# A filter's stored values in fp32, and its squares in a buffer of their own

## The reference

```python
x = x + _L0_conv_ref(_gn(x), w0, w1, w2, bias)   # 3 Haar levels, each a 5x5 convolution 128 -> 128 channels
x = x + _L1_conv_ref(_gn(x), spatial_weight)

# _L1_conv_ref: a 5x5 filter whose weights come from the image
dot = jnp.einsum('bchw,bckhw->bkhw', x, patches)
norm_x = jnp.sqrt(jnp.sum(x * x, axis=1))
norm_p = jnp.sqrt(jnp.sum(patches * patches, axis=1))
sim = dot / jnp.maximum(norm_x[:, None] * norm_p, EPS)
weight = (sim + 1.0) * 0.5 * spatial_weight[None, :, None, None]
out = jnp.einsum('bckhw,bkhw->bchw', patches, weight)
```

## Time and profile before

| | |
|---|---|
| median of 3 runs | 2229.93 us (2226.68 to 2234.81) |
| profiled execution | 2236.67 us, span 2235.0 us |
| busy of the span | PE 1634.4 us (73%), DVE 1408.0 (63%), ACT 738.2 (33%), POOL 448.3 (20%) |
| mean granted clock of PE | 0.829 of 2.4 GHz |
| DMA | 329.95 MB, mean 148 GB/s |

### The profile page before, as it was taken

One profiled execution on the slowest core, in us unless ns is written; L12 is line 12 of the kernel. 1 busy time (PEld: TensorE's weight loads), 2 busy tenths in 40 slices (PEclk: granted clock), 3 DMA queues, 4 the chain that ended last, 5 costly groups with the idle time before them and its releaser, 6 DMA issues.

```text
span 2235.0 us, 49426 instructions
## 1 busy us (share of the span) xinstructions
PE 1634.4 (73%) x16895; PEld 862.5 (39%) x16895; DVE 1408.0 (63%) x2121; ACT 738.2 (33%) x1222; POOL 448.3 (20%) x792
## 2 busy tenths in 40 slices
PE   5777777878578776888568785778678795875465
PEld 3543333434234343434234342335334352432243
DVE  6428646966378455966478554866479554875354
ACT  2321233423243233424233242423334242423341
POOL 1352422022301222012300232013300232011000
PEclk7888888989789897979788896989888896887566
DMA  5242446763857546673856556583766557572665
GB/s 164 75 125 75 122 129 152 185 171 92 192 141 192 140 126 167 157 186 99 189 149 183 134 133 167 140 207 99 172 162 174 139 131 178 139 197 76 146 164 135
DMA packets 151106, 329.95 MB, mean 148 GB/s; under 512 B 47092, under 2 KB 96244, under 8 KB 150260
## 3 DMA queue, kind: packets, MB, share of 16 engines
q1 hardware_dynamic: 109296, 207.18, 37.2%
q0 software_dynamic: 41472, 118.24, 20.1%
HBM read 238.70 MB, written 86.61 MB: 146 GB/s over the span
## 4 chain that ended last, share of the span: by engine, by line
PE 27%; DMA 21%; DVE 18%; SPq 17%; issue 11%; ACT 3%; DVEq 2%; POOL 0%; ACTq 0%; POOLq 0%
DMA d_n<-st_n 12%; PE conv L1300 8%; PE conv L1274 5%; DMA unit_mem<-d_n 5%; SPq L385 4%; DMA unit_mem<-d_hl 3%; SPq L413 3%; PE gram L1368 3%; PE conv L1259 3%; SPq L383 2%; PE out_ps L1393 2%; SPq L408 2%; SPq L405 2%; DVE wgt L1020 2%; PE stat_ps L1323 2%
## 5 line engine op out<-in xcount | busy, mean ns | idle before, releaser
L1020 DVE SCALAR_TENSOR_TENSOR wgt<-gram,tapw 124x512 f32<-124x512 f32 x512 | 350.4, 687 | 360.5 <-PE gram L1368 321.9
L1300 PE MATMUL conv<-thl,wconv 128*128 128x496 f16 (+2 forms) x1920 | 559.9, 422 | 16.8 <-DVE xa L899 9.6
L471 POOL DMA_DIRECT2D ring<-in_x x576 | 333.7, 584 | 475.3 <-DVE bn L781 244.1
L1368 PE MATMUL gram<-unit_mem 128*60 128x128 f16 x4096 | 264.8, 255 | 198.9 <-DMA unit_mem<-d_hl 122.8
L1368 PEld LDWEIGHTS gram<-unit_mem 128*60 128x60 f16 x4096 | 160.6, 118 | 428.9 <-issue 427.2
L1323 PE MATMUL stat_ps<-st_n,sq_c 128*128 128x306 f32 x256 | 123.0, 570 | 186.7 <-ACT st_n L556 153.7
L1300 PEld LDWEIGHTS conv<-thl,wconv 128*128 128x128 f16 x1920 | 171.2, 105 | 223.8 <-issue 81.3
L1274 PE MATMUL conv<-thl,wconv 128*128 128x480 f16 (+7 forms) x1200 | 255.3, 367 | 0.0
L1393 PE MATMUL out_ps<-wgt,vals 124*32 124x128 f32 x4096 | 195.2, 311 | 35.6 <-issue 31.5
L556 ACT ACTIVATE vals<-vals_ps 124x512 f32<-124x512 f32 x128 | 76.3, 596 | 391.5 <-PE vals_ps L1351 391.5
L505 POOL DMA_DIRECT2D up<-d_z x128 | 68.7, 539 | 560.4 <-DVE xa L951 500.5
(11 more groups left out here) (133 smaller groups left out, 2007.3 us busy)
## 6 DMA issues: line engine op xcount, KB each, us to landing
unit_mem<-d_hl SPq DMA_DIRECT2D x128, 360.0 KB, 6.5
unit_mem<-d_hl SPq DMA_DIRECT2D x256, 180.0 KB, 8.4
ring<-in_x POOLq DMA_DIRECT2D x288, 128.0 KB, 4.1
ring<-in_x POOLq DMA_DIRECT2D x288, 127.0 KB, 4.4
d_hl<-st_hl SPq DMA_DIRECT2D x128, 180.0 KB
d_v<-st_v SPq DMA_DIRECT2D x128, 180.0 KB
unit_mem<-d_v SPq DMA_DIRECT2D x64, 360.0 KB
up<-d_z POOLq DMA_DIRECT2D x160, 128.0 KB, 3.2
```

The lines of the kernel that those rows point to most:

```text
L471: pool.dma_start(dst, src).then_inc(raw_in[slot], 16)
L1020: V.scalar_tensor_tensor(out=dst, in0=g, scalar=SIM_SCALE ** 2, in1=tapw[:, :].unsqueeze(1).to_broadcast([KN, 2, 2 * QN]), op0=ALU.add, op ...
L1300: last = mm(dst[:, :, b0:b1], wconv0[:, w, 2 * (p % ROWS4) + s, dx + 2, :], thl[:, p % 2, d, s, :, b0 + dx:b1 + dx] if p % ROWS4 != 1 else ...
L1368: last = mm(bank[row:row + KQ, col:col + QN], key[:, q, e_at, TH * KW * g:TH * KW * g + KQ], tile[:, :, TH * g + 1:TH * g + 1 + TH, 1:1 + ...
```

## The change

The values go through memory once in fp32 in place of two fp16 parts: `st_v` and `d_v` are fp32, one DMA of 360 KB stores them and two DMAs load them, quadrants 0 and 1 to partitions 0 to 31 and quadrants 2 and 3 to partitions 32 to 63. The constant `pick_c` (fp32, 64x32 for each pair of quadrants, zero for the other pair) takes the place of `unpair_c`. DVE's `value_lows` is gone. The squares have a buffer of their own, `st_sq`, one for both parities; `half_in` no longer waits for the store but for `unit_low` of half h - 2; squaring is a function of its own, which waits until the matmuls of the half before have read `st_sq`; the wait for the store stands in `norms`, before the first write into `st_n`; the copy of the values follows in `norms` after the square of `st_a`. `xh2` and `xl2` now share memory with `thl`, so `wino_high(i, 0)` waits for the level-2 convolution.

```diff
-SAVES, LOADS, LATER = 80, 96, 80
+SAVES, LOADS, LATER = 64, 96, 96
...
-    unpair = np.zeros((2 * C, C), np.float16)
-    unpair[np.arange(2 * C), np.arange(2 * C) % C] = 1 / X_SCALE
+    pick = np.zeros((2 * C, 2, C), np.float32)
+    pick[np.arange(2 * C), np.arange(2 * C) // C, np.arange(2 * C) % C] = 1 / X_SCALE
...
+        xh2, xl2 = (thl[:, 0, hl, 0, 0:GR // 2, :].rearrange("p g w -> p (g w)").rearrange("p (h w) -> p h w", w=H2) for hl in range(2))
...
-        xh2, xl2 = sb("xh2", [P, H2, H2], F16), sb("xl2", [P, H2, H2], F16)
...
-        st_v = sb("st_v", [P, 2, 2, FN], F16)
+        st_v = sb("st_v", [P, 2, FN], F32)
...
+        st_sq = sb("st_sq", [P, UN], F32)
...
-                for hl in range(2):
-                    sp.dma_start(d_v[b, h, hl].rearrange("c q n -> q c n"), st_v[:, hl, h % 2, :]).then_inc(half_saved[h % 2], 16)
+                sp.dma_start(d_v[b, h].rearrange("c q n -> q c n"), st_v[:, h % 2, :]).then_inc(half_saved[h % 2], 16)
...
-                sp.dma_start(values[s][0:2 * C].rearrange("c q e n -> c (q e n)"),
-                             d_v[b, u].rearrange("l c q n -> (l c) (q n)")).then_inc(rest_in[s], 16)
+                for t in range(2):
+                    sp.dma_start(values[s][C * t:C * t + C].rearrange("c q e n -> c (q e n)"),
+                                 d_v[b, u, :, 2 * t:2 * t + 2, :].rearrange("c q n -> c (q n)")).then_inc(rest_in[s], 16)
...
             def wino_high(i, p):
                 act.wait_ge(t_wide, 8 * i + p + 1)
-                if p == 1:
-                    act.wait_ge(conv_ready, 3 * i + 3)
-                elif p or not first(i):
+                if p < 2:
+                    act.wait_ge(conv_ready, 3 * i + 1 + 2 * p)
+                if p >= 2:
                     act.wait_ge(m_ready, 16 * i + 2 * p - 2)
...
-                act.wait_ge(half_saved[half], START + SAVES * (4 * b + h // 2))
+                act.wait_ge(unit_low, START + 8 * b + (h - 1 if h >= 2 else 0))
...
                 last.then_inc(x2_done, 1)
+
+            def square_half(b, h):
                 act.wait_ge(x2_done, 8 * b + h + 1)
-                part = st_x2[:, half, :, :].rearrange("p h w -> p (h w)")
-                copy(st_n[:, half, :], part, scale=1 / X_SCALE, func=ACT.Square).then_inc(sq_done, 1)
-                copy(in_strips(st_v[:, 0, half, :]), strips(part)).then_inc(v_high, 1)
+                if h > 0:
+                    act.wait_ge(n2_ready, 16 * b + 2 * h)
+                copy(st_sq[:, :], st_x2[:, h % 2, :, :].rearrange("p h w -> p (h w)"), scale=1 / X_SCALE, func=ACT.Square)\
+                    .then_inc(sq_done, 1)
...
                 if p == 0:
                     act.wait_ge(unit_vec, START + 8 * b + h)
+                    act.wait_ge(half_saved[h % 2], START + SAVES * (4 * b + h // 2))
...
                     copy(st_b[:, :], st_a[:, :], func=ACT.Square).then_inc(root_squared, 1)
+                    copy(in_strips(st_v[:, h % 2, :]), strips(st_x2[:, h % 2, :, :].rearrange("p h w -> p (h w)"))).then_inc(v_kept, 1)
...
                     half_in(b, 0)
+                    square_half(b, 0)
                     half_in(b, 1)
...
                     norms(b, 0, 1)
+                    square_half(b, 1)
...
                     half_in(b, 2)
+                    square_half(b, 2)
...
                             half_in(b, j + AHEAD + 1)
+                            square_half(b, j + AHEAD + 1)
...
-                dve.wait_ge(value_low, 8 * b + h + 1)
+                dve.wait_ge(v_kept, 8 * b + h + 1)
...
-                mm(stat_ps[:, 0:PIECE], same_quadrant, st_n[:, h % 2, p * PIECE:(p + 1) * PIECE], start=True, stop=True)\
+                mm(stat_ps[:, 0:PIECE], same_quadrant, st_sq[:, p * PIECE:(p + 1) * PIECE], start=True, stop=True)\
...
-                                      values[s][0:2 * C, q, e, TH * KW * g:TH * KW * g + KQ], unpair_c[:, :],
+                                      values[s][0:2 * C, q % 2, e, TH * KW * g:TH * KW * g + KQ], pick_c[:, q // 2, :],
```

More of the change, by code:

```diff
@@ L130, in host_constants @@
             taps[64 * (k % 2):64 * (k % 2) + KQ, t, k // 2] = (dr == t // K - K // 2) & (dc == t % K - K // 2)
-    return square, gather, taps.reshape(KN, TAPS * 2 * QN), unpair
+    return square, gather, taps.reshape(KN, TAPS * 2 * QN), pick
 def first(n):
@@ L153, in link, with build @@
         engine.wait_ge(self.sem, self.base + self.k)
-def build(nc, x, w0, w1, w2, bias, spatial, square, gather, tapmask, unpair, out):
+def build(nc, x, w0, w1, w2, bias, spatial, square, gather, tapmask, pick, out):
     ctx = ExitStack()
@@ L196, in build @@
         gat_c = sb("gat_c", [P, Q, P], F32)
-        unpair_c = sb("unpair_c", [2 * C, C], F16)
+        pick_c = sb("pick_c", [2 * C, 2, C], F32)
         bn1, bn2 = sb("bn1", [P, CONV_TILES, 6], F32), sb("bn2", [P, CONV_TILES, 6], F32)
@@ L218, in unit_part @@
             return unit_mem[:, s, n * Q * FN:(n + 1) * Q * FN].rearrange("p (q e n) -> p q e n", q=Q, e=GROUPS)
-        keys, queries, values = ([unit_part(s, n) for s in range(2)] for n in range(3))
+        keys, queries = ([unit_part(s, n) for s in range(2)] for n in range(2))
+        values = [unit_mem[:, s, 2 * Q * FN:3 * Q * FN].bitcast(F32).rearrange("p (q e n) -> p q e n", q=2, e=GROUPS) for s in range(2)]
         norm_strips = [unit_mem[:, s, 2 * Q * FN:3 * Q * FN].bitcast(F32).rearrange("p (e n) -> p e n", e=2) for s in range(2)]
@@ L244, in build @@
         d_hl = dram("d_hl", [B, 2 * BANDS, 2, C, Q, FN], F16)
-        d_v = dram("d_v", [B, 2 * BANDS, 2, C, Q, FN], F16)
+        d_v = dram("d_v", [B, 2 * BANDS, C, Q, FN], F32)
         d_n = dram("d_n", [B, 2 * BANDS, Q, UN], F32)
@@ L298, in build @@
         sq_done = sem("sq_done")
-        v_high = sem("v_high")
+        v_kept = sem("v_kept")
         n2_ready = sem("n2_ready")
@@ L306, in build @@
         unit_high = sem("unit_high")
-        value_low = sem("value_low")
         unit_low = sem("unit_low")
@@ L372, in _ @@
             sp.dma_start(spat[:, :], spatial.rearrange("(a k) -> a k", a=1).to_broadcast([P, TAPS])).then_inc(const_in, 16)
-            sp.dma_start(unpair_c[:, :], unpair).then_inc(const_in, 16)
+            sp.dma_start(pick_c[:, :, :], pick).then_inc(const_in, 16)
             sp.wait_ge(wmixed, 7)
@@ L712, in iteration @@
                     half_in(b, 3)
+                    square_half(b, 3)
                 for j in range(CONV_TILES):
@@ L978, in units_close @@
                                        op0=ALU.mult, op1=ALU.mult).then_inc(unit_vec, 1)
-            def value_lows(b, h):
-                dve.wait_ge(v_high, 8 * b + h + 1)
-                V.tensor_tensor(in_strips(st_v[:, 1, h % 2, :]), strips(image_of(h)), in_strips(st_v[:, 0, h % 2, :]),
-                                ALU.subtract).then_inc(value_low, 1)
             def unit_lows(b, h):
                 dve.wait_ge(unit_high, 8 * b + h + 1)
-                dve.wait_ge(value_low, 8 * b + h + 1)
+                dve.wait_ge(v_kept, 8 * b + h + 1)
                 V.tensor_tensor(in_strips(st_hl[:, 1, h % 2, :]), strips(st_b[:, :]), in_strips(st_hl[:, 0, h % 2, :]), ALU.subtract).then_inc(unit_low, 1)
@@ L1079, in prepare @@
                     units_close(b, h)
-                    value_lows(b, h)
                     unit_lows(b, h)
@@ L1112, in iteration @@
                             if h < 2 * BANDS:
-                                if k == 0:
-                                    value_lows(b, h)
                                 if k == 3:
@@ L1542, in const_arrays @@
 def const_arrays():
-    return dict(zip(("square", "gather", "taps", "unpair"), host_constants()))
+    return dict(zip(("square", "gather", "taps", "pick"), host_constants()))
 _INS = ["x", "L0_conv_w0", "L0_conv_w1", "L0_conv_w2", "L0_conv_bias", "L1_conv_spatial_weight"]
```

## The result

| | median | ratio to before |
|---|---|---|
| before | 2231.93 us (2226.68 to 2234.81) | |
| after | 2256.18 us (2250.9 to 2261.56) | 1.0111 [1.0078, 1.0145] |

The profiled execution has a span of 2256.9 us, against 2235.0 before. I had forecast 2210 us; the change costs some 24 us where I expected it to give 20.

A forecast was written before the change was run, and what follows sets the result against it. No engine was taken to hold the chain; ScalarE's waits for d_n stores also stall TensorE and VectorE. Per pass -5.8 - 2.2 - 0.9 + 5.3 = -3.6 us, seven times -25, last image +4.5: -20, so 2210 us, range 2180 to 2242.

The forecast's parts named there:

- Part 1: Opening, half 4: store wait moves from half_in to norms; landing of store 2 to low(4) 16.9 us, gain 5.8 us.
- Part 2: Opening: the store of half 2 lands earlier, since value_lows and issues go and ring loads start sooner; 2.2 us together.
- Part 3: VectorE's value_lows, 56.8 us busy, goes; beyond low(0) only unit 2's is on the chain: -0.9 us a pass.
- Part 4: TensorE's fp32 value matmuls: +0.7 us a call at full clock, +1.6 at 1.2 GHz; +5.3 us a pass on the chain.
- My five calls: Value calls taken to be on the chain each pass: four in units 6 and 7, and the first of unit 4.
- If that cover fails, +0.7 us each: Part 4's proviso: calls in units 0 to 3 and 5 lie under VectorE, loads or stalls; otherwise each adds 0.7 us.
- Part 5: ScalarE: square and value copy keep their size, the copy moves, wino_high(0) gets a wait; cost 0.
- The last image: Image without convolutions: load starts 2.9 us sooner, calls in units 2, 4, 6 and 7 cost more; +4.5 us in all.
- The signs of being wrong: A warm call over 1.6 us, store 2 landing later than before, or unit 2's grams waiting for keys in every pass.
- the fourth: Rival: the change doesn't do what it says; the wait in norms binds as long as in half_in, gain 0; chance 0.02.
- The first: Rival: fp32 matmuls cost more than the stall gives back, turning at 1.0 us a warm call; 2258 us; chance 0.17.
- The second rival: DMA engines take the gain: earlier ring loads hold up store 1 by up to 4 us; 2242 us; chance 0.17.

The follow-up runs named there:

- experiments 8 and 9: Store of half 2 issued before load 1: 8 in the kernel with 16 merged matmuls a call, 2157.77 us; 9 in the changed kernel, 2246.74 us.
- experiment 7: Changed kernel with the four raw_stats of tile 0 at k = 4 to 7 instead of 0 to 3, so ring loads start later: 2251.15 us, 1.0097.
- experiment 3: Changed kernel with 16 fp32 matmuls a call instead of 32, each moving 64 columns: 2172.67 us, ratio 0.9729.
- the doubled kernels: Changed kernel with value matmuls issued twice in some units: units 0 and 1, 2284.34 us; 2 to 4, 2356.55 us; 5 to 7, 2343.75 us.

## Why the prediction was wrong, by its own steps

- **Part 1 (the waits move), right, a little small.** From the landing of store 2 to the end of low(4) I forecast 16.9 us; it is 15.2, so the gain in the pass shown is 7.5 and not 5.8. The wait at st_a was as described, but 17 times and 161.4 us, not 24 and 200.
- **Part 2 (when it lands), right in sign.** Store 2 landed 72.0 us after low(0) before and 70.6 now (1132.9 less 1062.3): 1.4 us earlier and 1.2 on average, 2.2 forecast. Parts 1 and 2 were to shorten the opening by 8.0 us, and 9.0 is the mean of seven passes. What lies behind this gate I had not looked for: experiments 8 and 9 take the wait for store 2 away and leave low(4) within 1 us (load 1 holds it in experiment 8), and in the changed kernel unit 2 waits for its keys.
- **Part 3 (value_lows), not seen by itself.** The 56.8 us are gone from VectorE (1408.0 to 1357.1 us busy). low(4) to low(5), where I put 0.9 us of gain, grew from 22.9 to 25.8 us; with 16 matmuls a call it is 22.3.
- **Part 4 (the fp32 matmuls) failed, and with it the sign.** First the price. I took the duration of one record for that of one matmul. Every fp32 matmul of this kernel stands in the trace as two records. It could be read in the rows ahead of the prediction: norm_piece issues 64 x 2 = 128 matmuls and its row says x256; filter_group issues 8 x 4 x 64 = 2048 and its row says x4096; the fp16 calls issue 4096 and their row says x4096. The median record is now

```profile
L1356 PEld LDWEIGHTS vals_ps<-pick_c,unit_mem x8192: 126/132/222, 330.2 to 2248.6; 64*60 64x60 f32 x200
L1356 PE MATMUL vals_ps<-pick_c,unit_mem x8192: 186/216/307, 330.2 to 2248.6; 64*60 64x32 f32 x200
```

132 ns for the weights, where I had 129, and 216 ns for the matmul, where I had 187: per record the estimate was fair. But there are 64 a call, so a call costs 1.88 - 0.58 = 1.3 us more at the full clock, where I had 0.7, and 3.35 - 0.96 = 2.4 at the low one, where I had 1.6. Then the count. My five calls at these prices are 3 x 1.3 + 2 x 2.4 = 8.7 us, and with the 8.9 us gained the pass would have come out level. Measured from low(4) on is +11.1 us, where I had +5.3 and part 3's -0.9: the chain has up to ten calls, since units 2 to 4 became bound by TensorE. "If that cover fails, +0.7 us each" was the right sentence with the wrong weight; it failed because of the length of the calls themselves. Between my +4.4 us from low(4) on (+5.3 and -0.9) and the +11.1 measured lie 6.7 us: 3.4 are the price of the five calls (8.7 in place of 5.3), 3.3 what the cover was to hold, with unit 2's wait for its keys and the stops inside calls in it. For units 6 and 7 the new price gives 3 x 1.3 + 2.4 = 6.3 us, and from low(7) on it was 6.4; between low(4) and low(7) the calls that I counted give 2.4 - 0.9 = 1.5, and it was 4.7.
- **Part 5 (ScalarE at nothing)**: its moves show no cost in the rest of the pass with 16 matmuls a call (157.7 us, 158.1 before). low(0) to low(1) is 8.2 us where it was 7.4, in every kernel with the squares apart or fp32 values; that is 0.8 us in the opening that I had at zero.
- **The last image**: forecast +4.5, measured +6.2.
- **The signs of being wrong**: of the three that I named, two came, a call of over 1.6 us at the full clock (1.88) and unit 2's grams waiting for their keys in every pass; the landing of store 2 did not come later. The chances that I wrote down add up to 0.98 for the forecast and three rivals, since the 0.02 of the fourth was put inside the second.
- **The rivals.** The first, fp32 matmuls that cost more than the stall gives back, is what happened. Its turning point of 1.0 us a warm call was right for the sign, and at c = 1.3 its formula gives 7 x (9.9 - 8.9) + 16.9 - 4.7 = +19 us, close to the +24 measured. Part of that is luck: it puts 7 us on the seven passes and 12 on the last image, where 14.6 and 6.2 were measured. I gave it 0.17 because weight load and matmul rows were far from four times fp16; they were, per record. By the Trainium skill (FP8 and Floating Point Precision, TensorE Precision Notes) true FP32 makes four passes; the trace shows two records a matmul and a call of 3.2 times the time (1.88 over 0.58), so that page's rule came nearer than my sum: four times would be 2.3 us, an estimate from that page's passes and the 0.58 us of the fp16 call. The Trainium skill (Perfetto Trace Analysis, section Engine Utilization) halves TensorE's output rate for FP32_LOW_HIGH; the two records a matmul would agree with that factor, though no row names the form in which these matmuls run, and the time grew 3.2 times and not twice. The second rival falls: the ring's earlier loads moved the landing of store 1 by 0.5 us (experiment 7), and without them the total stays the same. That the change doesn't do what it says falls too.

What stays open: which part of 29 against 18 ns a record is the weight load; why the rest of the pass gains 2.3 us in experiment 8; what unit 2's wait for its keys costs by itself; and why the chain takes in ten calls in some passes and seven or eight in others (a loss of 17.3 us in one, 3.7 in another). That the calls are the cause is shown by experiment 3; which of them count is read from the chain of single passes and from the doubled kernels.

## What to carry to other kernels

Before pricing a change of type by rows of the same type elsewhere in the trace, divide a row's count by the number of instructions in the code: the row's duration is for a record, and here an fp32 matmul was two. For the many small matmuls here the number of records was the price, so let one move more columns: 32 more columns cost 6 ns, a matmul saved 59. And count covered work at its new length: calls that lay under another engine at 0.58 us were on the chain at 1.88.

A stall that is removed uncovers the next gate. Here load 1 stood close behind store 2, and taking the wait for store 2 away left low(4) where it was; and where the opening got shorter, the keys of unit 2 came too late.

## What the runs showed that I had not expected

- Each fp32 matmul of 64x60 by 64x32 occupied TensorE for 59 ns at the full clock (1.88 us / 32), the fp16 one for 18; with 64 columns moved it was 65 ns (1.04 us / 16).
- fp32 values alone cost the last image 17.6 us (194.8 against 177.2), the changed kernel 6.2: a loss of the calls and the gain of the waits meet there too, though no convolutions run beside the filter.
- In the changed kernel 17 calls of 64 records stop before their last 9, 15 or 6, for 0.3 to 5.2 us, with "issue" as what ended it; in the group's row above these are the 45.3 us. 32.0 of them stand in the second call of unit 0 (55 + 9), 4.0 to 5.2 us in all seven passes:

```profile
1119.55 0.71 PE L1356 MATMUL vals_ps<-pick_c,unit_mem 64*60 64x32 f32 x9 [4.83 <-issue]
```

The kernel with 16 matmuls a call has none of them (its matmul group stood idle for 0.0 us). The opening is no longer with the stops in unit 0 (84.8 us) than without them (85.6), so these cost nothing there. The other 13.3 us, 8.5 of them in the first call of unit 6 in five passes, can be part of the loss after low(4). They come at a few fixed places of the program; what ends them is not in the profile, and the cause stays open.
- Issuing the d_n store took 8.19 us in a row of before; in the changed kernel the slow issue of the same store is the values' DMA:

```profile
1117.41 3.28 SPq L387 DMA_DIRECT2D d_v<-st_v  x1
1120.89 1.88 SPq L388 DMA_DIRECT2D d_n<-st_n  x1
```

The same 9.6 KB store took 0.57 us to issue for half 0 and 4.85 us for half 1 of this pass, so its own bytes don't set the time; what does isn't in these rows.
- The best kernel found has the squares in their own buffer, fp32 values and 16 merged matmuls a call: 0.9729 [0.9684, 0.9775] of the time before, 0.9688 [0.963, 0.9746] with store 2 issued early.
